# Second layer of a graph network: the order of the features in the normalised rows

## What is computed

```python
def _L0_ffn_ref(x, phi, scale, w1, b1, w2, b2):      # x: (1, 6250, 768), phi: (768, 32, 32)
    xn = _l2norm(x, axis=2)
    phin = scale * _l2norm(phi, axis=0)
    logits = jnp.einsum('bld,des->bles', xn, phin)
    d_w = softmax(logits, axis=-1)                     # per expert, over its slots
    c_w = softmax(logits.reshape(b, l, E * S), axis=-1)
    slots = jnp.einsum('bld,bles->besd', xn, d_w)
    h = gelu(jnp.einsum('besd,edh->besh', slots, w1) + b1[:, None, :])
    eo = jnp.einsum('besh,ehd->besd', h, w2) + b2[:, None, :]
    return jnp.einsum('bkd,blk->bld', eo.reshape(b, E * S, d), c_w)

x = x + gnn(layernorm(x), ...)
x = x + _L0_ffn_ref(layernorm(x), ...)
```

## Time and profile before

| | us |
|---|---|
| median of 3 runs | 3398.9 (3392.09 to 3399.05) |
| span of the profiled execution | 3527.4 |
| TensorE (PE) busy in it | 3143.9 (89%) |
| weight loads (PEld) | 2019.7 (57%) |
| VectorE (DVE) | 1942.6 (55%) |
| ScalarE (ACT) | 1205.6 (34%) |
| GpSimd (POOL) | 1842.0 (52%) |

### The profile page before, as it was taken

One profiled execution on the slowest core, in us unless ns is written; L12 is line 12 of the kernel. 1 busy time (PEld: TensorE's weight loads), 2 busy tenths in 40 slices (PEclk: granted clock), 3 DMA queues, 4 the chain that ended last, 5 costly groups with the idle time before them and its releaser, 6 DMA issues. The chain is left out here.

```text
span 3527.4 us, 56846 instructions
## 1 busy us (share of the span) xinstructions
PE 3143.9 (89%) x19474; PEld 2019.7 (57%) x19474; DVE 1942.6 (55%) x2983; ACT 1205.6 (34%) x1447; POOL 1842.0 (52%) x1754
## 2 busy tenths in 40 slices
PE   7237999999999999967999999999999998588998
PEld 7125666666666666634665656665656664244665
DVE  8773444444443444425777877777777775101332
ACT  6951222222222222213444444444444442011000
POOL 0146666666666666536676666776666661100000
PEclk9999999999999999979999999999999999799999
DMA  9488888888888888749998988988889987999996
GB/s 374 180 316 317 293 280 287 303 287 271 298 284 299 293 295 297 263 159 312 313 307 291 311 298 297 312 302 294 288 286 308 308 284 287 340 324 271 277 268 177
DMA packets 344441, 1018.61 MB, mean 289 GB/s; under 512 B 145314, under 2 KB 148668, under 8 KB 335984
## 3 DMA queue, kind: packets, MB, share of 16 engines
q0 software_dynamic: 135776, 660.85, 56.5%
q1 hardware_dynamic: 196916, 322.85, 27.3%
q10 hardware_dynamic: 11484, 31.39, 2.8%
HBM read 854.14 MB, written 135.08 MB: 280 GB/s over the span
## 5 line engine op out<-in xcount | busy, mean ns | idle before, releaser
L1299 POOL DMA_INDIRECT xs<-table,idx x833 | 914.2, 1097 | 501.3 <-PE m_part L1476 214.0
L821 POOL DMA_INDIRECT xs<-table,idx x833 | 878.8, 1055 | 442.9 <-issue 202.9
L1073 PE MATMUL a_part<-xs 128*128 128x512 f16 (+1 forms) x3332 | 592.1, 332 | 76.1 <-DMA xs<-table,idx 52.5
L1476 PE MATMUL m_part<-xs 128*128 128x512 f16 (+1 forms) x3332 | 591.9, 332 | 55.7 <-DMA xs<-table,idx 19.2
L1053 PE MATMUL a_ps_o<-Ws,xs 128*128 128x512 f16 x3528 | 593.1, 326 | 8.9 <-issue 5.5
L1073 PEld LDWEIGHTS a_part<-xs 128*128 128x128 f16 x3332 | 416.3, 142 | 213.2 <-issue 96.9
L1476 PEld LDWEIGHTS m_part<-xs 128*128 128x128 f16 x3332 | 419.3, 142 | 198.4 <-issue 77.3
L1053 PEld LDWEIGHTS a_ps_o<-Ws,xs 128*128 128x128 f16 x3528 | 344.9, 98 | 236.8 <-issue 12.6
L1505 PE MATMUL m_ps_l<-xs,m_xT 128*128 128x512 f16 x1764 | 391.6, 380 | 8.0 <-issue 7.9
L1492 PE MATMUL m_ps_s<-dw_mem,xn_mem 128*128 128x512 f16 x1296 | 312.2, 380 | 3.5 <-DVE xs L1365 3.0
L1505 PEld LDWEIGHTS m_ps_l<-xs,m_xT 128*128 128x128 f16 x1764 | 172.2, 98 | 219.2 <-issue 16.8
(11 more groups left out here) (377 smaller groups left out, 3770.9 us busy)
## 6 DMA issues: line engine op xcount, KB each, us to landing
xs<-in_L_ffn_w_dram SPq DMA_DIRECT2D x64, 1152.0 KB, 11.3
xs<-table SPq DMA_DIRECT2D x98, 384.0 KB
xs<-table,idx POOLq DMA_INDIRECT x1666
cw_dram<-xs SPq DMA_DIRECT2D x49, 512.0 KB
x_pad<-xs SPq DMA_DIRECT2D x7, 2688.0 KB, 23.9
table<-arena SPq DMA_DIRECT2D x49, 384.0 KB, 4.5
table<-xs SPq DMA_DIRECT2D x49, 384.0 KB
xs<-x_pad SPq DMA_DIRECT2D x49, 384.0 KB
```

The lines of the kernel that those rows point to most:

```text
L821: pool.indirect_dma_start(out=ring[:, t, :], out_offset=None, in_=table, in_offset=bass.IndirectOffsetOnAxis(ap=idx[:, k:k + 1], axis=0)). ...
L1073: mm = nc.tensor.matmul(part[:, bass.ds(to + a, z - a)], pick[:, i % 2, :, t], ring[:, n % RING, half * D + a:half * D + z], start=False, ...
L1299: pool.indirect_dma_start(out=ring[:, t, :], out_offset=None, in_=table, in_offset=bass.IndirectOffsetOnAxis(ap=idx[:, n:n + 1], axis=0)). ...
L1476: mm = nc.tensor.matmul(part[:, bass.ds(off + at, e - f)], pick[:, i % 2, :, t], ring[:, n % RING, half * D + f:half * D + e], start=False ...
```

## The change

Three things change together. ScalarE writes `xn` and `tmp` in the order of the slots' features: it reads `xb` through `spread` (element 6d + c) and writes it at c*128 + d, contiguous (`grouped`, a new helper). phi is loaded as (p c), so its chunks hold the same features. The units and the late units take their chunk of `xn` as 128 consecutive elements. The low half follows from `tmp` and `xn` as before.

```diff
@@ first_layer, sync
                     if i == SQ_AT - 1:
                         sp.wait_ge(lo1, 1)
-                        sp.dma_start(phi_f[:, :, :], phi.rearrange("(c p) e s -> p c (e s)", p=P)).then_inc(p_in, 16)
+                        sp.dma_start(phi_f[:, :, :], phi.rearrange("(p c) e s -> p c (e s)", p=P)).then_inc(p_in, 16)
@@
+def grouped(rows, n):
+
+    return rows.rearrange("p (c d) -> p c d", c=n)
+
+
 def spread(rows, n):
 
     return rows.rearrange("p (d c) -> p c d", c=n)
@@ second_layer, scalar
-                        nc.scalar.activation(xn[j % XN][:, 0, :], xb[:, j % 2, :], ACT.Identity, bias=xc[:, 0:1], scale=xf[:, 0:1]).then_inc(xn_hi, 1)
-                        nc.scalar.activation(tmp[:, :], xb[:, j % 2, :], ACT.Identity, bias=xc[:, 0:1], scale=xf[:, 0:1]).then_inc(xn_f, 1)
+                        nc.scalar.activation(grouped(xn[j % XN][:, 0, :], DC), spread(xb[:, j % 2, :], DC), ACT.Identity, bias=xc[:, 0:1], scale=xf[:, 0:1]).then_inc(xn_hi, 1)
+                        nc.scalar.activation(grouped(tmp[:, :], DC), spread(xb[:, j % 2, :], DC), ACT.Identity, bias=xc[:, 0:1], scale=xf[:, 0:1]).then_inc(xn_f, 1)
@@ second_layer, tensor, unit
-                                mm = nc.tensor.matmul(ps_s[:, tile % 2, :], spread(xn[q % XN][:, xh, :], DC)[:, c, :], dw[:, q % DW, dh, a:a + 512],
+                                mm = nc.tensor.matmul(ps_s[:, tile % 2, :], xn[q % XN][:, xh, c * P:(c + 1) * P], dw[:, q % DW, dh, a:a + 512],
@@ mixture, tensor, late_unit
-                            mm = nc.tensor.matmul(ps_o[:, c % 2, 0:K // 2], spread(xn[b % XN][:, xh, :], DC)[:, c, :], dw[:, b % DW, dh, K // 2:K],
+                            mm = nc.tensor.matmul(ps_o[:, c % 2, 0:K // 2], xn[b % XN][:, xh, c * P:(c + 1) * P], dw[:, b % DW, dh, K // 2:K],
```

## The result

The changed kernel takes 3407.09 us (median of 11 runs, 3400.28 to 3412.97), the kernel before in the same series 3396.14 us (11 runs, 3392.09 to 3402.07). The ratio is 1.0027, with a 95% interval of 1.0017 to 1.0037: about 9 us slower, between 6 and 13.

What follows compares the result with a forecast made beforehand. TensorE's stream of columns was taken as the bound in the steady part. Weights 0, ScalarE's stepped reads +6.3 and phi 0 summed to +6 us, from 3398.9 to 3405 us (+0.18%), range 3388 to 3424.

Steps and rivals of the forecast that it cites:

- (a): Dispatch weights at L1492 and L1927: loads fall from 125 to 98 ns, hidden beside 216 ns matmuls; gain 0.
- (b): ScalarE's stepped reads at L1326 and L1327: +0.45 us each, delay paid whole in seven bins without gap, +6.3 us.
- upper end: ScalarE's stepped activations: twice the time, +1.0 us each, as the far side of the weight loads' trend.
- lower end: ScalarE's stepped activations: no extra time, since about 1.05 ns an element was called far slower than stepped weight reads.
- The 5.0 us of the middle: 10 further bins with short gaps: 5.0 us together, counted only into the range; late signals suspected to come from profiling.
- Rival of ScalarE at twice the time: L1326 and L1327 +1.0 us each, 2.0 on the chain: 14 to 43 us more, about 3420 us; chance 0.14.
- (c): phi's load, 24 KB a partition in one run: value 0, bounds -5 to +5 us.
- Rival out: phi's load alone decides, by the gathers beside it: 3394 to 3404 us; chance 0.11.

Runs made afterwards that it cites:

- e1: Kernel before with only the weights of units and late units read as 128 consecutive elements: 3398.5 us, ratio 0.9996.
- e2: Changed kernel with weights read at step 6 and phi loaded as before, leaving only ScalarE's stepped reads: 3405.37 us, ratio 1.0019.
- e10: Changed kernel with ScalarE's stepped reads in bins 0 to 3, 47 and 48 alone, contiguous elsewhere: 3404.82 us, ratio 1.0022.
- e11: Changed kernel with ScalarE's stepped reads in bins 4 to 46 alone, contiguous elsewhere: 3399.09 us, ratio 1.0007.
- e4: Changed kernel with tmp written first by the one stepped read, then the float16 rows copied contiguously from tmp: 3400.14 us, ratio 1.0006.
- e7: Changed kernel with ScalarE reading xb contiguous and writing with a step, on the slower chip: 3654.13 us, ratio 1.0328.
- e9: Kernel before, unchanged, profiled again: span 3400.6 us; timed beside it 3397.74 us.
- e3: Kernel before with only phi loaded as (p c), 24 KB a partition in one run: 3398.1 us, ratio 1.0000.
- e6: Changed kernel with stepped reads in bins 4 to 46 alone, on the chip where the kernel before takes 3534.79 us: 3548.48 us, ratio 1.0038.
- e12: Changed kernel with one more contiguous ScalarE activation ahead of xn_f in every bin: 3426.49 us, ratio 1.0090.

## Why the prediction was right, and where it was not

The forecast was +6 us; +9 (6 to 13) was measured. Point by point:

- **(a), weights with unit step, 0 on the path.** Right. 125 to 98 ns as forecast, the pace unchanged, e1 at 0.9996. What decided it was the pace of matmuls by starts, not the share of PEld.
- **(b), place of the loss.** Right: the chain L1326, L1327, L1427, L1433, L1330, L1334, L1527, paid where TensorE already waits at L1527 (e2, e10), and nothing of it in the middle that can be measured (e11).
- **(b), how it is paid.** Only the last bin pays as forecast, the delay whole: its wait at L1527 grows from 2.6 to 4.1 us and the period by 1.5. The three bins of the fill do not. TensorE's clock has no term in the forecast, and it is most of what they lose: about 6.1 us by the comparison with e4, where the transposes are as late and the clock stays up. Without the lower clock the waits for gathers behind L1527 could have taken up most of the delay. No run changes the clock alone, so the 6.1 us is an estimate, from two kernels that differ in ScalarE's second write as well.
- **(b), size of one activation.** Mis-sized: +0.45 us each was taken from the weight loads' ratio, +0.78 and +0.76 were measured, 1.75 times as long. That lies nearer to the upper end (twice) than to the value taken. The weight loads were a poor neighbour for another engine's reads of wider elements. The argument for the lower end was wrong as well: 1.05 ns an element is not far slower than the 0.98 and 1.1 ns of the stepped loads. Here the Trainium skill came nearer. The figure of "Vector Engine (DVE) Microarchitecture Reference", 5.2, that the prediction used gave an estimate of 1.1 us for both; the trace has 1.55. That figure is for steps of 72 and 152 words; the same table has 2.50 ns a column for a step of 24 words, nearer to the 6 words here, which would make an estimate of 2 x 768 x 1.45 ns = 2.2 us. The measured value lies between the two. The note that two accesses must fall in a 16-byte line for full rate (the Trainium skill, "SBUF — State Buffer", Specifications (TRN2)) agrees in sign: 24 bytes between elements cost 0.78 us / 768 = 1.0 ns an element. The sentence of the Trainium skill's "ScalarE: Activation LUTs", one element per cycle for every function, fits the contiguous activations of this trace and neither the stepped reads (1.81 us) nor the stepped writes (e7, up to 3.83 us).
- **(b), number of bins.** Seven were counted; it is four. The clean profile of the kernel before has gaps of 5.5, 0.14, 0.14 and 0.14 us in bins 0 to 3, and bin 48 has 0.14; bins 41 and 42 have more than 1.67. Bin 0 has room in every clean profile (3.8 to 7.2 us in e9, e1, e3 and e11, 1.0 still in the changed kernel). 4 x 1.55 = 6.2 us is close to the forecast's 7 x 0.9 = 6.3, but that is luck twice over: the size was too small and the bins too many, and the fill's share is not a sum of delays at all. The profiles place 7.4 us, 5.9 in the fill and 1.5 in the last bin; the rest up to the measured 9 is inside the interval.
- **The 5.0 us of the middle, left out of the sum.** Leaving them out was right; the reason given was not. The late signals don't come from profiling: the profiled execution e9 has none, and on the chip where the *timed* runs of the kernel before take 3535 us, the profiles have them. The profile ahead of the prediction, with its 3527.4 us, was of that kind, the timed runs beside it of the other. In that slower condition the middle seems to pay (e6, 1.0038, of which its profile places 4.8 us there), about what was left out. What makes the signals late there stays open.
- **Rival of ScalarE at twice the time.** By size it nearly came true (1.75 times), but it would have been priced at 14 to 43 us, again from the disturbed gaps. With the clean ones it decides in the median bin only beyond 2.0 us on the chain, and e12 with 2.56 shows it: 29 us.
- **(c), phi.** 0, as forecast (e3). Rival out.

## What to carry to other kernels

When an operand's order is wrong for one engine, look where the step is paid for: here it cost TensorE nothing, as the load ran beside a matmul longer than itself, and cost ScalarE 0.77 us an instruction. A delay on a chain beside a saturated engine is paid only in the fill and the drain; count those bins, and read the smallest gap in the steady part to see how much more it bears. In the bins that pay, don't stop at the wait: other waits behind it (here for gathers) can absorb the delay, and a longer stand of TensorE can cost clock on top. Read the granted clock of the stretch behind the wait in both profiles. Two shorter waits can be much cheaper than one of the same sum, as e4 shows. A profiled span that differs from the timed median by several per cent is a warning: gaps read in it may be those of another condition.

## What was not expected of the hardware

ScalarE reading float32 24 bytes apart takes 1.81 us for 768 columns instead of 1.03. Writing float16 256 bytes apart takes 3.83 us, while float32 512 bytes apart takes 1.86. Waits of 3.3 to 3.6 us in one piece sent TensorE on at a clock of 0.54 to 0.68 for the next 5 us, while 9.9 us of waits in pieces of at most 2.2 left the clock behind the second transposes at 1.00. Loading 3 MB in runs of 24 KB beside the gathers landed 3 us sooner than in runs of 4 KB. The same kernel took 3397 us on some chips and 3535 us on another, at about the same granted clock (0.97 to 0.98), with late signals from TensorE in the slower case alone.
